# Graph attention on one core: shared gathers right behind a tile's own in GpSimd's list, and ten places of its own per row instead of eleven

## What is computed

```
h    = relu(layernorm(x))                       # sources
hs   = layernorm(h) * scale1 + bias1            # 2048 x 256
ht   = layernorm(h_target) * scale1 + bias1
q    = (ht @ Wq + bq) / sqrt(32);  k = hs @ Wk + bk;  v = hs @ Wv + bv
logits = where(adj != 0, q . k per head, -1e30)
ctx  = softmax(logits) @ v
y    = layernorm(ht + ctx @ Wo + bo) * scale2 + bias2
out  = x + y + gelu(y @ W1) @ W2
```

## Time and profile before

| | |
|---|---|
| median of 3 runs | 394.51 us (394.04 to 395.02) |
| the profiled execution | 395.59 us, of which 393.9 us from its first to its last instruction (the span) |
| PE, DVE, POOL, ACT busy | 86%, 76%, 61%, 43% of the span |

### The profile page before, as it was taken

How to read it: one execution, slowest core, us unless ns; L and a number is a source line. 1 busy time by engine, 2 the same in 40 slices (tenths; PEclk the granted TensorE clock), 3 DMA queues, 4 the chain that set the end, 5 groups by cost and what they waited for, 6 DMA issues and landing times.

```text
span 393.9 us, 5345 instructions
## 1 busy us (share of the span) xinstructions
PE 337.4 (86%) x1654; PEld 280.3 (71%) x1654; DVE 300.6 (76%) x678; ACT 170.1 (43%) x407; POOL 238.8 (61%) x303
## 2 busy tenths in 40 slices
PE   3999988427742959999899999999999989999984
PEld 1688877226532648887688778788887878888873
DVE  5977894598915989889889998999999595762210
ACT  4999664301303244716343571653435245243210
POOL 6654047777777777787777778777777771200100
PEclk9999999859695869999999999999999999999998
DMA  7996977778878565756666583646447351101000
GB/s 231 298 272 202 254 253 248 228 263 238 197 246 235 141 185 139 217 126 179 184 190 173 138 241 106 188 131 196 136 129 236 94 171 47 41 0 53 2 27 31
DMA packets 31158, 65.64 MB, mean 167 GB/s; under 512 B 5370, under 2 KB 15894, under 8 KB 31128
## 3 DMA queue, kind: packets, MB, share of 16 engines
q0 software_dynamic: 17696, 49.27, 46.0%
q1 hardware_dynamic: 13408, 15.99, 12.0%
q10 hardware_dynamic: 24, 0.01, 0.0%
HBM read 76.82 MB, written 6.29 MB: 211 GB/s over the span
## 4 chain that ended last, share of the span: by engine, by line
POOL 28%; PE 28%; DVE 22%; issue 13%; DMA 6%; ACT 1%; POOLq 1%; DVEq 0%; ACTq 0%
POOL near L540 25%; DVE logits L1119 7%; PE turned L1534 6%; DMA near<-kv_saved,far_index 5%; PE wide L1520 5%; PE lines L1476 4%; PE lines L1351 3%; PE turned L1352 3%; DVE near L1108 2%; PE small L1398 1%; POOL rstd_y L485 1%; PE wide L1325 1%; PE turned L1497 1%; DVE stats L862 1%; DVE values L1137 1%
## 5 line engine op out<-in xcount | busy, mean ns | idle before, releaser
L540 POOL DMA_INDIRECT near<-kv_saved,index x176 | 177.0, 1006 | 56.5 <-issue 54.4
L1476 PE MATMUL lines<-values,ident 128*128 128x264 f32 x352 | 86.0, 403 | 9.2 <-DVE values L1137 8.1
L1476 PEld LDWEIGHTS lines<-values,ident 128*128 128x128 f32 x352 | 68.8, 199 | 23.5 <-issue 11.6
L1520 PE MATMUL wide<-yT,w 128*128 128x256 f32 x256 | 61.0, 389 | 0.0
L1534 PE MATMUL turned<-w,hidden 128*128 128x256 f32 x256 | 58.5, 382 | 2.2 <-DVE result L1160 1.9
L1108 DVE TENSOR_TENSOR near<-near,lines 128x2816 f32<-128x2816 f32 x16 | 49.3, 3079 | 10.3 <-DMA near<-kv_saved,index 10.3
L1137 DVE TENSOR_TENSOR values<-near,small 128x3072 f32<-128x3072 f32 x16 | 53.6, 3350 | 2.5 <-ACT small L723 2.5
L1534 PEld LDWEIGHTS turned<-w,hidden 128*128 128x128 f32 x256 | 47.5, 190 | 10.4 <-DVE result L1160 4.5
L1119 DVE TENSOR_REDUCE logits<-near 128x96 f32<-128x3072 f32 x16 | 53.6, 3353 | 0.0
L1520 PEld LDWEIGHTS wide<-yT,w 128*128 128x128 f32 x256 | 48.8, 195 | 6.3
L736 ACT ACTIVATE context<-lines,sums_inverse 128x32 f32<-128x32 f32 x128 | 24.6, 307 | 54.1 <-DVE sums_inverse L1144 54.1
(11 more groups left out here) (148 smaller groups left out, 527.8 us busy)
## 6 DMA issues: line engine op xcount, KB each, us to landing
adjacency<-in_adj POOLq DMA_DIRECT2D x16, 512.0 KB, 7.5
kv_saved<-kv_out SPq DMA_DIRECT2D x3, 1024.0 KB, 6.5
near<-kv_saved,index POOLq DMA_INDIRECT x176, 3.7
ht<-in_L_gnn_h_target SPq DMA_DIRECT2D x4, 512.0 KB, 18.2
w<-in_L_gnn_W SPq DMA_DIRECT2D x2, 1024.0 KB, 8.7
xr<-in_x SPq DMA_DIRECT2D x8, 256.0 KB, 4.6
out<-result SPq DMA_DIRECT2D x8, 256.0 KB, 3.3
xs<-in_x SPq DMA_DIRECT2D x3, 512.0 KB, 6.9
```

The source lines that it names most:

```text
L540: pool.indirect_dma_start(out=near[:, n % RING, s, :], out_offset=None, in_=kv_saved, in_offset=bass.IndirectOffsetOnAxis(ap=ids.bitcast(U ...
L1476: pe.matmul(acc, ident[:], values[:, s, :], start=(s == 0), stop=False)
L1520: mm = pe.matmul(wide[:, f % 2, half * 2 * P:(half + 1) * 2 * P], w1[:, d, fs], yT[:, e % 2, d, :], start=(d == 0), stop=(d == DC - 1))
```

## The change

`SLOTS` is 10 instead of 11, so a tile has ten own transfers and one shared. In GpSimd's list the shared transfer of a tile stands right behind its own ones, with only a `load_adj` between them; before, ten or more own transfers of the next tile stood in between. The adjacency of tile m is loaded beside the gathers of tile m-5 instead of m-6, and `root_pair` stands behind the shared transfer of the odd tile. The code behind GpSimd's part moves up by seven lines.

```diff
-SLOTS = 11
+SLOTS = 10
...
-        FIRST_ADJ = 7
+        FIRST_ADJ = 5
...
             gather(1, range(PLACES))
-            for n in range(0, ST + 1, 2):
-                if 0 < n < ST:
-                    free_ring(n + 1)
-                    gather(n + 1, range(SLOTS))
-                    gather(n, (SLOTS,))
-                if n + FIRST_ADJ < ST:
-                    load_adj(n + FIRST_ADJ)
-                if n + 2 < ST:
-                    free_ring(n + 2)
-                    gather(n + 2, range(SLOTS))
-                if n + 1 + FIRST_ADJ < ST:
-                    load_adj(n + 1 + FIRST_ADJ)
-                e = normed_in(n)
-                if e is not None:
-                    root_pair(e)
-                if 0 < n < ST:
-                    gather(n + 1, (SLOTS,))
+            for n in range(2, ST + 1, 2):
+                for m in (n, n + 1):
+                    if m < ST:
+                        free_ring(m)
+                        gather(m, range(SLOTS))
+                    if m + FIRST_ADJ < ST:
+                        load_adj(m + FIRST_ADJ)
+                    if m < ST:
+                        gather(m, (SLOTS,))
+                root_pair(normed_in(n))
```

## The result

The changed kernel takes 364.72 us (364.07 to 365.32, 4 runs) against 394.49: 29.8 us less, ratio 0.9245, interval 0.9223 to 0.9266. Forecast were 372.8 us in a range of 367 to 379. The direction was right and the size too small by 8 us, outside the range.

What follows compares the result with a forecast made beforehand. GpSimd was taken to bound the start, GpSimd, DVE and PE about level from round 3, PE the end. Terms -16.3 - 4.0 - 1.4 = -21.7 us took the median from 394.5 to 372.8 us, range 367 to 379.

Steps and rivals of the forecast that it cites:

- Term one: Start up to round 3: earlier shared transfers let round 3 start at 120.5 instead of 136.85, -16.3 us.
- The 0.7 us added for TensorE: Ahead of round 3: the next pair's words come after round 1's sum on TensorE, so 0.7 us was added.
- the fourth loop: Rounds 3 to 13: `root_pair` waits for an even round's measurement, own transfers follow; 30.1 to 32.4 us a pair.
- Term two: Rounds 3 to 13: five pairs at 33.0 us each, 165 against 169, -4.0 us (bounds 0 and -8.0).
- Term three: The end, from 305.87 on: PE binds and three sums shrink by 0.46 us each, -1.4 us.
- TensorE's gaps closing: Rival, rounds 3 to 13 and end: pairs at 32.2 us, end 1 us better, 367.8 us; chance 0.14.
- The load in front of the shared transfer: Rival, GpSimd's pairs: the adjacency load holds the shared transfer up, about 401 us at its longest; chance 0.03.
- Late adjacency: Rival, at the start: adjacency or words late, or PE longer at its lower clock, 381 us; chance 0.05.
- The wait for `take_shared` on GpSimd: Even tiles' shared transfers wait for the round before's `take_shared`; 4 us of cover, costed at nothing.

Runs made afterwards that it cites:

- the start alone: Kernel before with eleven own places and the old order, only the shared transfers of tiles 2 and 3 moved right behind their own: 393.57 us.
- the places alone: Kernel before with ten own places instead of eleven (`SLOTS = 10`), old order of GpSimd's list kept: 379.07 us.
- the order alone: Changed kernel with eleven own places (`SLOTS = 11`), so only the new order of GpSimd's list: 382.56 us.
- two cuts together: Changed kernel with one product fewer in each TensorE sum and DVE's first wide product over seven of ten own places: 361.00 us.

## Why the prediction was wrong in size

**Term one held.** -17.2 against -16.3, about 0.1 beyond its bound of -17.1; the steps (round 2 at 103.6, shared operation at 106.4, no wait for the index) came out at 103.28 and 106.24. The 0.7 us added for TensorE was not needed. The path named was right but not complete: that `root_pair` now stands ahead of tile 4's own transfers was counted as a cost of the fourth loop, and not as what keeps the gain, without which the start alone gives nothing.

**Term two is the step that failed**: "I take 33.0 us a pair" and "5 x 33.0 = 165 against 169". It measured 159.9: 9.2 less instead of 4.0, beyond even the bound of 8.0. 33.0 is a whole pair's length, put against 33.8, a mean over five of which the last has no adjacency left to sort: 29.1 before, 27.7 after. That alone is 5.3 us too much (33.0 for 27.7). The three middle pairs, at 32.43, were sized 0.6 too long each, 1.7 us in all, since I had left TensorE the gaps that it had and they closed to 0.2; the first, 34.83, was sized 1.8 too short. In that one TensorE, after it had stood mostly idle, had half its full clock granted for 5 us, the lower of its two levels (1.2 GHz), and DVE waits three times, 0.76, 2.16 and 0.96 us:

```profile
119.64:125.00 5.36, 1.28 (x9) 0.81 (x7) 5.36 (x5) 2.14 (x9) 4.03 (x5) 0.99 0.66 170
125.00:130.00 5.00, 4.33 (x13) 3.61 (x14) 4.83 (x14) 2.81 (x9) 3.90 (x4) 0.50 0.64 188
```

The prediction put no price on the clock in this stretch; what it costs was not measured by itself. The bound for DVE, worked out from 33.85 of one whole pair instead of the mean, would have been 33.85 - 1.68 = 32.2, and the longer wait for the words (1.01 against 0.75) makes 32.4. That pairs differ could be read from the earlier trace rows: from 242.35 to 305.87 two pairs take 63.5 us, 31.8 each, against 33.85 for the one before them.

**Term three**: "three sums go" and "PE is busy all the time, so they give nothing more". It measured -4.1 against -1.4. Behind the start of round 13 lie four sums and not three, since TensorE's sum of round 12 begins there (at 304.97, 0.9 us ahead): 1.8 us. And PE was not busy all the time. Its gaps up to the last sum fell from 1.04 to 0.06, and before they stood in round 13, behind the wait for the shared transfer that was said to give nothing, here on DVE and on TensorE:

```profile
312.91 0.42 DVE L1112 TENSOR_TENSOR near<-near,lines 128x256 f32<-128x256 f32 x1 [3.98 <-DMA near<-kv_saved,far_index]
```
```profile
316.23 0.44 PE L1488 MATMUL turned<-ident,context 128*128 128x128 f32 x2 [0.47 <-ACT context L736]
318.94 0.71 PE L1494 MATMUL turned<-ident,ht 128*128 128x128 f32 x4 [0.54 <-ACT context_T L768]
```

ACT's context needs a reciprocal that stands behind L1112 in DVE's list. With the places alone, where DVE still waits 3.62 us in that round, the two gaps are 0.28 and 0.23. Of the rest, 0.4 lies behind TensorE's last instruction, 0.2 is only where DVE's round 13 lies against TensorE's sum, and some 0.6 is not taken apart. In the kernel with the places alone the end gave 2.6, in that with the order alone 0.8.

**The rivals.** The one nearest to the outcome, TensorE's gaps closing, 367.8 at 0.14, was right in kind. It used the same faulty mean, and its reason was only half right, since TensorE alone did not bind. The load in front of the shared transfer does delay it, by about 1.5 us at the median, far from the 12 us that the rival needed, and it cost no time. Late adjacency did not come true. The wait for `take_shared` on GpSimd, costed at nothing with 4 us of cover, is nothing here, and grows to 9 or 10 us as soon as root_pair comes late.

## What to carry to other kernels

When a stage is forecast per round, size each round by its own rows: a mean over rounds of unlike content, put against the length of a full one, was the larger part of this error. When several engines stand within a few per cent, cutting one tells little; cut two and three together, and look for small waits that stay when an engine's work shrinks. In a list issued in order, what stands ahead of a long run of transfers matters beyond its own cost: one line of four small operations, moved behind ten transfers, turned 364.7 us into 415.5.

## What had not been expected of the hardware

An indirect gather of 128 rows that was issued 0.9 us behind a 512 KB load landed in 4.9 us at the median, against 3.3 with that load issued behind it.

The same kernel before took medians of 475.0 and 483.6 us on two chips and 393.9 to 394.5 in all other measurements. The first of the two and the one with 393.9 (in the run of two cuts together, 73 minutes later) have the same chip number, 3, so it need not be a lasting property of that chip. In the traces from these two (the order alone) GpSimd, DVE, ACT and TensorE all stand idle longer and more often, for a part without a wait that the trace explains. The parts' ratios from these two measurements could not be used. The cause stays open.
